# A recurrent stage re-ordered: one unit's inputs on GpSimd, the heads' inverse root in two third-order steps

## The reference, cut to what matters

```python
xa = _ln(x, ln1_w, ln1_b); sx = shifted(xa) - xa
xxx = tanh((xa + sx * maa_x) @ maa_w1)           # five low-rank mixes
xk, xw, xv, xr, xg = xa + sx * (maa_stack + xxx @ maa_w2)
w = exp(-exp(time_decay + tanh(xw @ td_w1) @ td_w2))
r, k, v = xr @ Wr.T, xk @ Wk.T, xv @ Wv.T; g = silu(xg @ Wg.T)
def step(s, rkvw):                                # over the 128 tokens
    a = k_t[..., :, None] * v_t[..., None, :]
    out = einsum('bhi,bhij->bhj', r_t, u * a + s)
    return a + w_t[..., :, None] * s, out
og = (out - mean) / sqrt(var + 1e-05)             # per head of 16
x1 = x + (og * gn_w + gn_b) * g @ Wo.T
xc = _ln(x1, ln2_w, ln2_b); xk2, xr2 = mixes(xc)
return x1 + sigmoid(xr2 @ Wfr.T) * (square(relu(xk2 @ Wfk.T)) @ Wfv.T)
```

## Time and profile before

| what | value |
|---|---|
| median of the runs shown | 3461.31 us (3460.58 to 3463.86) |
| the profiled execution's own time | 3457.59 us |
| its span, first to last instruction | 3455.8 us |
| busy in the span | PE 3175.1, DVE 1776.9, ACT 1160.8, POOL 793.3 us |
| recurrent stage, first to last scan | 1613.5 to 2411.3 us |

### The profile page before, as it was taken

One profiled execution on the slowest core, in us unless ns is written; L12 is line 12 of the kernel. 1 busy time (PEld: TensorE's weight loads), 2 busy tenths in 40 slices (PEclk: granted clock), 3 DMA queues, 4 the chain that ended last, 5 costly groups with the idle time before them and its releaser, 6 DMA issues. The chain is left out here.

```text
span 3455.8 us, 52394 instructions
## 1 busy us (share of the span) xinstructions
PE 3175.1 (92%) x19136; PEld 2078.5 (60%) x19136; DVE 1776.9 (51%) x2577; ACT 1160.8 (34%) x4083; POOL 793.3 (23%) x565
## 2 busy tenths in 40 slices
PE   7999899989999888886899999997799999899999
PEld 5666566657676655555666666664355555567675
DVE  4655455510000178874899999998254544400000
ACT  2444233421111266661333443342233333311111
POOL 2333233310000012222444444445000000100000
PEclk9999999989999999998899999998999999999999
DMA  4110231110000131112111111110130110101000
GB/s 166 42 46 27 80 131 52 40 64 22 15 21 17 42 150 47 49 39 68 35 51 38 37 49 37 41 43 28 64 133 26 36 41 20 49 22 33 21 33 12
DMA packets 104307, 170.17 MB, mean 49 GB/s; under 512 B 16512, under 2 KB 54016, under 8 KB 100736
## 3 DMA queue, kind: packets, MB, share of 16 engines
q1 hardware_dynamic: 99296, 124.58, 11.4%
q10 hardware_dynamic: 4896, 44.04, 3.1%
HBM read 135.03 MB, written 33.55 MB: 49 GB/s over the span
## 5 line engine op out<-in xcount | busy, mean ns | idle before, releaser
L2386 POOL TENSOR_TENSOR rec_S<-rec_S,rec_r_t 128x1024 f32<-128x1024 f32 x128 | 302.0, 2359 | 362.4 <-DVE rec_S L2686 362.3
L2686 DVE TENSOR_TENSOR_SCAN rec_S<-rec_decay,rec_S 128x1024 f32<-128x1024 f32 x128 | 318.0, 2484 | 5.8 <-ACT rec_S L2446 1.5
L2076 PE MATMUL mlp_bank<-mlp_src_t,region_a 128*128 128x256 f32 x1024 | 224.1, 382 | 3.1 <-ACT mlp_src_t L1997 3.1
L2076 PE MATMUL pmlp_bank<-pmlp_src_t,region_a 128*128 128x256 f32 x1024 | 224.7, 382 | 1.9 <-ACT pmlp_src_t L1997 1.9
L2088 PE MATMUL pmlp_bank<-region_a,pmlp_h_t 128*128 128x512 f32 x512 | 221.1, 593 | 0.0
L2088 PE MATMUL mlp_bank<-region_a,mlp_h_t 128*128 128x512 f32 x512 | 221.1, 593 | 0.0
L2076 PEld LDWEIGHTS mlp_bank<-mlp_src_t,region_a 128*128 128x128 f32 x1024 | 196.2, 192 | 32.9 <-issue 6.8
L2076 PEld LDWEIGHTS pmlp_bank<-pmlp_src_t,region_a 128*128 128x128 f32 x1024 | 196.6, 192 | 31.7 <-issue 5.5
L1505 ACT ACTIVATE group_scores<-group_scores,group_negmax 128x128 f32<-128x128 f32 x512 | 197.6, 392 | 28.4 <-DVE group_negmax L1599 18.5
L2043 DVE TENSOR_TENSOR mlp_y<-mlp_bank,mlp_xres 128x512 f32<-128x512 f32 x16 | 11.1, 692 | 374.2 <-PE mlp_bank L2088 374.2
L2043 DVE TENSOR_TENSOR pmlp_y<-pmlp_bank,pmlp_xres 128x512 f32<-128x512 f32 x16 | 11.1, 692 | 363.5 <-PE pmlp_bank L2088 363.5
(11 more groups left out here) (366 smaller groups left out, 6495.1 us busy)
## 6 DMA issues: line engine op xcount, KB each, us to landing
rec_vb<-v_by_head SPq DMA_DIRECT2D x32, 512.0 KB, 4.2
region_a<-in_C_w ACTq DMA_DIRECT2D x2, 4096.0 KB, 18.8
region_a<-in_G_w ACTq DMA_DIRECT2D x2, 4096.0 KB, 18.0
self_xres<-in_x SPq DMA_DIRECT2D x16, 256.0 KB, 2.6
rows_A<-self_xres SPq DMA_DIRECT2D x16, 256.0 KB, 2.0
cross_ctx_t<-in_ctx_t SPq DMA_DIRECT2D x16, 256.0 KB, 3.3
cross_xres<-rows_A SPq DMA_DIRECT2D x16, 256.0 KB, 2.6
rows_B<-cross_xres SPq DMA_DIRECT2D x16, 256.0 KB, 2.0
```

Source lines behind the costliest of these rows:

```text
L2076: product = nc.tensor.matmul(ph.bank(item)[:, i * TT:(i + 1) * TT], W1[:, c, f:f + 128], src_t[:, c, :, :], start=c == 0, stop=c == C - 1)
L2386: nc.gpsimd.tensor_tensor(S[u % 4][:, :, :], S[u % 4][:, :, :], bcast(r_t[:, s.k, UNITS[u][0], :], [128, JH, T], 1), ALU.mult)\
L2686: nc.vector.tensor_tensor_scan(St[:, :, :].rearrange(flat), decay[m][:, :, :].rearrange(flat), St[:, :, :].rearrange(flat), 0.0, ALU.mult, ...
```

## The change

- **Inputs of unit 4** move from DVE (`inputs(middle, 4)`) to POOL (`inputs_half`, after `multiply_states(middle, 3)`). POOL reads k from a new SBUF copy `k_sb` that ACT makes (`keys_copy`). The scan of unit 4 waits for `a4_done`. DVE now counts 7 inputs a sequence (`NA`).
- **Head root**: two steps of third order instead of three Newton steps; the chain has 10 operations instead of 11. One of them, `(ha - 10/3) * ha`, has both inputs in SBUF; a scale of 9/64 is folded into `head_norm`.
- **Bonus**: `bonus_products` is done at the end of the step of `front` instead of in the middle of the step of `middle`; PE's `bonus` follows the mixes 1 and 2 of the next step, its bank is another one (`n`), the copy comes earlier on ACT, and `bonus_values` stands before `multiply_states(middle, 2)` instead of after unit 6.
- **Norm statistics**: DVE no longer negates the mean (two small operations a step); POOL does, ahead of its power.
- **Order**: DVE gathers before mix 1, and adds the residual before the tail's output. PE does one more chunk of `ffn_gate(tail)` and the transposes before `sum_heads(back, 7)`. ACT's `normalise_front(ahead)` moves ahead of `shifted_back(back)`. POOL's `rsqrt` for `ahead` moves ahead of `multiply_states(middle, 5)`.
- **Buffers**: `x1` is doubled, `xn2` no longer shares with `y` (it shares with `sq`), so `normalise_back` doesn't wait for the store; `sigmoid_tanh` does.
- **Start of the stage**: PE transposes the first rows, and ACT copies them, before they wait for the weights and the setup.

```diff
             def rsqrt(n, tile, out, var_done, out_done):
                 pool.wait_ge(var_done, n + 1)
+                nc.gpsimd.tensor_tensor(out[:, 2:3], tile[:, 6:7], minus_one[:, :], ALU.mult)
                 nc.gpsimd.tensor_tensor(out[:, 0:1], tile[:, 9:10], minus_half[:, 0:1], ALU.pow).then_inc(out_done, 1)
+            def inputs_half(s):
+                pool.wait_ge(vb_loaded[1], s.n * 16 + 16)
+                pool.wait_ge(k0_done, s.n + 1)
+                pool.wait_ge(reduced, s.n * NU + 1)
+                nc.gpsimd.tensor_tensor(S[0][:, :, 1:T], vb[1][:, :, 0:T - 1],
+                                        bcast(k_sb[:, 0:T - 1], [128, JH, T - 1], 1), ALU.mult).then_inc(a4_done, 1)
...
                 if middle:
+                    bonus_values(middle)
                     multiply_states(middle, 2)
                 if middle:
                     multiply_states(middle, 3)
+                    inputs_half(middle)
                 if back:
                     rsqrt(back.n, stats2, rstd2, back_norm[2], rstd2_done)
                 if middle:
                     multiply_states(middle, 4)
-                if middle:
-                    multiply_states(middle, 5)
                 if ahead and not is_first(ahead.n):
                     rsqrt(ahead.n - 1, stats, rstd, front_norm[2], rstd_done)
                 if middle:
+                    multiply_states(middle, 5)
                     multiply_states(middle, 6)
-                    bonus_values(middle)
...
+            def keys_copy(s):
+                act.wait_ge(k_full, s.n + 1)
+                wait_count(act, a4_done, s.n)
+                nc.scalar.copy(k_sb[:, :], k_bank[s.k][:, 0:T]).then_inc(k0_done, 1)
...
                 if back:
                     normalise_back(back)
                 if front:
+                    keys_copy(front)
                     receptance(front)
+                if ahead and not is_first(ahead.n):
+                    normalise_front(ahead)
                 if back:
                     shifted_back(back)
...
-                nc.vector.tensor_scalar(tile[:, 8:9], tile[:, 6:7], -1.0, None, ALU.mult)
...
+                for i, square in enumerate((1.0, 9 / 64)):
+                    dve.wait_ge(root_step, at + 4 * i + 2)
+                    nc.vector.scalar_tensor_tensor(hb, hv, square, hy, ALU.mult, ALU.mult).then_inc(root_step, 1)
+                    dve.wait_ge(root_step, at + 4 * i + 3)
+                    nc.vector.tensor_tensor(ha, hb, hy, ALU.mult).then_inc(root_step, 1)
+                    dve.wait_ge(root_step, at + 4 * i + 4)
+                    nc.vector.scalar_tensor_tensor(hb, ha, -10 / 3, ha, ALU.add, ALU.mult).then_inc(root_step, 1)
+                    dve.wait_ge(root_step, at + 4 * i + 5)
+                    if i == 0:
+                        nc.vector.scalar_tensor_tensor(hy, hb, 5.0, hy, ALU.add, ALU.mult).then_inc(root_step, 1)
...
                     scan(middle, 0)
+                if back:
+                    gather(back)
                 if front:
                     mix(front, 1)
-                if back:
-                    gather(back)
...
+                if back:
+                    residual(back)
                 if tail:
                     output(tail)
-                if middle:
-                    inputs(middle, 4)
-                if back:
-                    residual(back)
                 if middle:
                     scan(middle, 4)
                 if front:
                     mix(front, 4)
+                if ahead and not is_first(ahead.n):
+                    stats_front(ahead)
                 if middle:
                     inputs(middle, 5)
                     scan(middle, 5)
-                    bonus_products(middle)
...
+                if front:
+                    bonus_products(front)
...
                 if front:
                     low_rank(front)
+                if tail:
+                    ffn_gate(tail, 1)
+                if front:
+                    low_rank_t(front)
                 if back:
                     sum_heads(back, NU - 1)
-                if front:
-                    low_rank_t(front)
                 if tail:
                     ffn_gate(tail, 2)
                 if front:
                     mix_pair(front, 1, 2)
+                if middle:
+                    bonus(middle)
                 if tail:
                     ffn_gate(tail, 3)
```

95 lines of the change are left out of this document (48 added, 47 removed), and 4 rows, old and new, of the table banks.

## The result

The changed kernel takes 3427.52 us in the median of four runs (3420.91 to 3430.35), the kernel before 3461.93 us beside it: a ratio of 0.990, with a 95% interval of 0.9886 to 0.9914. The forecast was 3426 us. The profiled run, the fastest of the four, took 3420.91 us; its span is 3419.1 us, against 3455.8 before. Behind the recurrent stage nothing has changed: from the last scan's end to the end of the span it is 1044.3 us, before 1044.5.

A forecast was written before the change was run, and what follows sets the result against it. DVE was taken as the first limit, PE 1.65 us a step behind. Steady steps -30.0, the next -2.4, start -2, first two recurrent steps -1, drain 0: -35.4, so a median of 3426 us, range 3410 to 3453.

The forecast's parts named there:

- Scan 4 to scan 0: Leg of the steady step from scan 4 to the next scan 0: from 21.1 to 20.3 us.
- Scan 0 to scan 1: Leg of the steady step: from 7.64 to 6.45 us, with PE late next.
- Scan 1 to scan 2: Leg of the steady step with the root chain: from 8.23 to 8.1 us.
- one less: -0.22: Scan 1 to scan 2: one operation fewer in DVE's root chain saves 0.22 us.
- Scan 2 to scan 4: Leg of the steady step that loses inputs 4 from DVE: from 13.61 to 13.0 us.
- The 0.25 us: Allowance for small waits in a steady step: legs sum to 47.85 us, 48.1 taken.
- Rival A: Head root: POOL's bonus holds a two-SBUF-input operation about 1.2 us; step 49.3, total 3442 us; chance 0.17.
- Rival B: ACT's order turns a short POOL delay at scan 5 long; step 50.6 to 51.1, 3458 to 3470 us; chance 0.13.
- Rival C: Unit 4's inputs on POOL cost DVE their whole 2.36 us; step 50.5, total 3457 us; chance 0.03.
- Rival D: DVE's charged waits for PE partly vanish; step 47.2, total 3414 us; chance 0.12.
- The start: Start of the stage: first transposes and copies run before the setup wait, -2 us (0 to -3).
- The drain: End of the stage: bonus out of the way, fewer operations, but a POOL wait; 0 us (+2 to -3).

The follow-up runs named there:

- e6: Changed kernel with all parts of the bonus back where they stood before the change: 48.73 us a steady step, 3435.7 us.
- e5: Changed kernel with the old head root in three second-order steps: 48.22 us a steady step, 3425.3 us.
- e1: Changed kernel with the inputs of unit 4 back on DVE, between mix 3 and the residual: 48.73 us a steady step, 3436.9 us.
- e2: Changed kernel with POOL's bonus product ahead of the first columns, beside the head root: 48.89 us a steady step, 3435.4 us.
- e3: Changed kernel with one extra POOL power of 0.54 us ahead of the rstd for `ahead`: 51.03 us a steady step, 3460.7 us.
- e11: Changed kernel with DVE's first output product ahead of the residual: 48.07 us a steady step, 3425.5 us.
- e7: Changed kernel with ACT's `normalise_front(ahead)` moved behind the first decay of the next chunk: 48.22 us a steady step, 3421.4 us.
- e9: Changed kernel with both the extra POOL power of 0.54 us and ACT's norm behind the decay: 48.22 us a steady step, 3424.0 us.
- e8: Kernel before with only the inputs of unit 4 moved to POOL: 49.73 us a steady step, 3448.3 us.
- e10: Changed kernel with PE's transposes of the next rows ahead of unit 5's head sums: 48.21 us a steady step, 3428.3 us.

## Why the prediction was right, point by point

- **The bound.** DVE was the first limit and PE 1.65 us behind it. The 2.65 us taken from DVE turned that round, and 2.42 us of them came through.
- **Scan 4 to scan 0**, forecast 20.3, measured 20.5. Scan 7 is down from 3.06 to 2.29 us and scan 5 from 2.60 to 2.29, as forecast. e6 confirms the first by putting it back. Scan 6 is now at 2.40, since it starts (1790.45) before POOL's product of unit 5 is over (1790.70); that wasn't in the sum.
- **Scan 0 to scan 1**, forecast 6.45, measured 6.26. Mix 1 no longer waits. The wait for PE's mean at the centring is 0.22 instead of the 0.35 in the sum and the 0.6 named among the signs. PE's terms of this leg add up to 5.9 us, not to the 5.8 written; from unit 7's head sum to the end of the mean it is 5.6 in the trace.
- **Scan 1 to scan 2**, forecast 8.1, measured 8.23. Here the step that failed is "one less: -0.22". It took DVE's chain for the bound, with 0.1 for the transposed root. It had worked out that PE is late up to scan 1 and didn't follow the same queue on to scan 2. e5 shows the term is zero in the steady steps.
- **Scan 2 to scan 4**, forecast 13.0, measured 13.1 and 13.35. The residual waits 0.64 us in one step and 0.43 in the next, forecast 0.5 to 0.6; the cover of the inputs is 0.67 and 0.42, forecast 0.5. Gain and wait together, 1.12 - 0.6, are the 0.52 of e1.
- **The 0.25 us** added to 47.85 for small waits was about right: the step is 48.21.
- **Rival A** (the root held by the bonus) missed the steady steps by 0.22 us, and struck in the last step (1.67 us, e5). Its mechanism is real (e2): 32 elements are enough. That agrees with the Trainium skill (SBUF — State Buffer, Who interferes with whom), whose rule goes by the order of issue and not by the shape of the operation. Its price was 0.68 us a step in e2 (for the first of the two operations) and not 1.2.
- **Rival B** (the order on ACT) didn't happen in the steady steps and did in the first full one. The edge was put at 0.35 us and lies at 0.43; a step beyond it takes 51.0 us in the mean of e3, forecast 50.6 to 51.1; 0.3 of it stands where the clock fell and not in the rival's chain.
- **Rival C** (POOL work costs DVE its own length) is out: by it the inputs on POOL would have been worth less than nothing, and taking them back (e1) costs 0.52 us a step. The residual, the statistics and the output beside the 2.35 us of inputs take 0.69 to 0.70 us each, as elsewhere. The warning of the Trainium skill (Perfetto Trace Analysis, Optimizing Scalar/DVE Operations) that such a move "might not help" doesn't hold for this place, where no instruction of DVE has two inputs in SBUF.
- **Rival D** (PE and DVE mesh better, 47.2 us) didn't happen: PE is still idle 2.5 us a step, and DVE's waits of 0.22, 0.30, 0.29 and 0.43 to 0.64 us for it remain. In e11 the last of them is gone, and a step is 47.7.
- **The start**, forecast -2. PE's first transposes begin at 1571.42 instead of 1574.16. The first scan of the changed kernel starts at 1608.85, 4.6 us earlier than before, but in the profiles of the eleven kernels with the same start it comes at 1611.1 to 1618.2, 1615.2 in the mean, later than the 1613.49 of before. Between 1570 and 1608 us the granted clock is 0.90 in the changed kernel's profile, 0.77 in that of before and 0.64 to 0.78 in the eleven. So that this part gains anything isn't shown. The -31.9 us of the stage don't depend on it. That the profiled run came within 1.1 us of its forecast of 3422 is partly luck: its 4.6 us of start, where -2 was forecast, make up for the stage, which gained 1.5 less than forecast.
- **The drain**, forecast 0, measured +1.35. By gaps: 0→1 -1.36, 1→2 +1.67, 3→4 +1.51, 5→6 -0.46. The +1.67 is rival A. The first and the third vary between kernels whose order is the same there. The gap 0→1 is 5.73 us in the changed kernel, e7 and e9, where the granted clock in it is 1.00, and 7.1 to 7.4 in the kernel before and nine others, where it is 0.76 or 0.77 (e8: 8.23 us at 0.59). The gap 3→4 is 7.6 to 9.5 us over all kernels, at a clock of 0.69 to 0.87 in it; in the changed kernel the residual waits 3.40 us there for PE, in e7 2.30. Why is open. The whole step is 44.3 to 47.3 us in the kernels with the changed order.
- Of the parts, the inputs (-0.52) and the bonus (-0.52) are measured by taking them out, the root is 0. The other 1.4 of the 2.42 us a step isn't isolated by a run. That gather ahead of mix 1 took away the wait of 1.01 us, and what the order of the statistics gave, is read from the timeline alone; and gather did it only together with the bonus, since in e6, which has it ahead too, mix 1 waits 0.59 us.

## What to carry to other kernels

Work out, for each engine, from where to where it runs without a gap: a saving on another engine inside such a stretch is worth nothing (e5), and so is filling the engine's idle time ahead of the event that starts the stretch (e10). Ahead of moving work to a slack engine, ask which of its small instructions then comes within half a microsecond of a long one that locks it out, and what waits in order behind that instruction on a third engine; reordering there costs nothing and takes the edge away (e9). The value of an edit depends on the order around it, here 0.91 or 0.52 us for the same product, so it is to be measured in both. And a collision that the steady steps miss by 0.22 us can still happen in the first and last ones: read those too.
